# Cross-attention in a decoder layer: each projection in two halves, between the head pairs of twelve steps

## The reference

```python
q = einsum('oc,bct->bot', Wq, target) + bq      # target = layernorm(x), per batch 256 x 512
k = einsum('oc,bcs->bos', Wk, source) + bk      # source = ctx
v = einsum('oc,bcs->bos', Wv, source) + bv
dot = einsum('bhdt,bhds->bhts', q, k) / sqrt(16)
dot = mask * dot - (1 - mask) * 1e6
amap = softmax(dot, axis=-1) * mask
out = einsum('bhts,bhds->bhdt', amap, v)
x = x + out
```

## Time and profile before

| | us |
|---|---|
| median of 3 runs | 2342.87 (2342.37 to 2356.09) |
| profiled execution | 2321.17 |
| its span | 2319.4, mean granted clock 0.963 |
| PE busy | 2162.2 (93%) |
| DVE busy | 1597.9 (69%) |
| ACT busy | 797.5 (34%) |
| POOL busy | 759.0 (33%) |

### The profile page before, as it was taken

One profiled execution on the slowest core, in us unless ns is written; L12 is line 12 of the kernel. 1 busy time (PEld: TensorE's weight loads), 2 busy tenths in 40 slices (PEclk: granted clock), 3 DMA queues, 4 the chain that ended last, 5 costly groups with the idle time before them and its releaser, 6 DMA issues. The chain is left out here.

```text
span 2319.4 us, 35373 instructions
## 1 busy us (share of the span) xinstructions
PE 2162.2 (93%) x11638; PEld 1521.2 (66%) x11638; DVE 1597.9 (69%) x2873; ACT 797.5 (34%) x1843; POOL 759.0 (33%) x531
## 2 busy tenths in 40 slices
PE   6899999999999999999999998879899989789998
PEld 4677777777777777777777876423333333267776
DVE  7658878878876558878888875657867878542221
ACT  1223323323323333223323322235555556652221
POOL 3234335335345234334335333212122221122211
PEclk9899999999999999999999999888978998999999
DMA  5211011011012111011011004745565444311100
GB/s 205 80 48 52 15 51 51 16 49 51 16 49 100 56 47 53 7 58 51 9 56 51 26 10 72 121 79 98 103 104 97 68 91 80 101 59 55 55 36 19
DMA packets 58564, 141.87 MB, mean 61 GB/s; under 512 B 9022, under 2 KB 23558, under 8 KB 53478
## 3 DMA queue, kind: packets, MB, share of 16 engines
q1 hardware_dynamic: 56726, 138.42, 23.7%
q10 hardware_dynamic: 1744, 2.25, 0.3%
HBM read 89.53 MB, written 17.29 MB: 46 GB/s over the span
## 5 line engine op out<-in xcount | busy, mean ns | idle before, releaser
L1638 DVE TENSOR_REDUCE x_mx<-x_pm 128x1 f32<-128x512 f32 x512 | 317.6, 682 | 77.3 <-PE x_pm L1731 74.4
L1493 ACT ACTIVATE x_E<-x_pd 128x512 f32<-128x512 f32 x512 | 265.0, 603 | 178.4 <-PE x_pd L1745 177.3
L1091 PE MATMUL a_pj<-q_big,a_wqk_h 128*128 128x512 f32 x1024 | 290.0, 405 | 0.5 <-POOL a_wqk_l L631 0.5
L1107 PE MATMUL a_pj<-a_wvg_h,q_big 128*128 128x512 f32 x1024 | 285.6, 406 | 1.1 <-DVE a_rm L789 1.0
L1107 PEld LDWEIGHTS a_pj<-a_wvg_h,q_big 128*128 128x128 f32 x1024 | 185.2, 188 | 51.8 <-DVE a_rm L789 2.4
L789 DVE TENSOR_TENSOR a_rm<-a_pj,a_rope 128x1024 f32<-128x1024 f32 x128 | 155.7, 1218 | 78.8 <-PE a_pj L1091 77.5
L1091 PEld LDWEIGHTS a_pj<-q_big,a_wqk_h 128*128 128x128 f32 x1024 | 183.0, 188 | 40.3 <-POOL a_wqk_l L631 1.3
L520 ACT ACTIVATE a_v<-a_pj 128x256 f32<-128x256 f32 x128 | 49.2, 384 | 414.8 <-PE a_pj L1107 414.8
L663 POOL TENSOR_TENSOR a_ogl<-a_ogf,a_ogh 128x512 fp32r<-128x512 f32 x62 | 79.3, 1302 | 281.8 <-ACT a_ogf L557 281.8
L1759 PE MATMUL x_pa<-x_E,x_vx 128*32 128x512 f32 x1024 | 154.3, 678 | 0.0
L866 DVE TENSOR_TENSOR a_acc<-a_po,a_acc 128x512 f32<-128x512 f32 x128 | 86.0, 687 | 88.6 <-PE a_po L1220 88.6
(11 more groups left out here) (220 smaller groups left out, 4618.4 us busy)
## 6 DMA issues: line engine op xcount, KB each, us to landing
a_qk_raw<-in_wqk SPq DMA_DIRECT2D x16, 1024.0 KB, 5.3
a_vg_raw<-in_wvg SPq DMA_DIRECT2D x16, 1024.0 KB, 4.9
a_wo_raw<-in_wo SPq DMA_DIRECT2D x16, 512.0 KB, 3.6
x_Q<-x_hi SPq DMA_DIRECT2D x20, 256.0 KB
x_K<-x_hi SPq DMA_DIRECT2D x20, 256.0 KB
a_acc<-in_w SPq DMA_DIRECT2D x6, 704.0 KB, 4.3
a_wt<-in_w SPq DMA_DIRECT2D x24, 176.0 KB, 2.3
weights_scratch<-a_wt SPq DMA_DIRECT2D x24, 176.0 KB, 1.9
```

The lines of the kernel that those rows point to most:

```text
L1091: last = mm(pj[:, j % 2, :], wa[:, c, j * P:(j + 1) * P], xa[:, c, p * UT:(p + 1) * UT], start=k == 0, stop=k == 11)
L1107: last = mm(pj[:, tt % 2, :], xa[:, c, t0:t0 + P], wa[:, c, :], start=k == 0, stop=k == 11)
L1493: nc.scalar.activation(E[:, n % ESLOTS, :], pd[:, n % 3, :], ACT.Exp, scale=XD ** -0.5).then_inc(exp_done, 1)
L1638: nc.vector.reduce_max(mx[:, u % 2, at:at + 1], pm[:, k % 3, :], AX_X).then_inc(pm_done, 1)
```

## The change

- A projection is made in two parts (`project_part`, k = 0 and 1: for K and Q each is one of the two accumulated input tiles, for V one half of the columns). The twelve parts stand in steps 4 to 15, between the first two row scores and the second two dots.
- PE's `turn_max` goes behind the first two row scores of a quad instead of ahead of them, and the numbering of pm's banks follows. In DVE's step the maxima are taken two and two, with `max_rows` and `take_projection` between them. `take_projection` is in the odd steps 5 to 15.
- `norm_stats` goes to step 1, `norm` to step 6. `high` goes to steps 6, 8, 10 and 12, in the middle of the four exponentials.
- Inversions: one part a step, in steps 0, 2, 3, 4, 8, 10, 12 and 14 (n = 2b - 2 in steps 0 and 2, n = 2b - 1 in steps 3 to 10, n = 2b in steps 12 and 14).
- SP: x of the first three batches is loaded ahead of the loop and before the fills; x of batch b + 3 in step 15; the context of b + 2 in step 1; the fills run from step 9 to step 1 of the next batch (LATE has two); for batch 1 only the six fills of Q stand ahead of the loop, those of K in steps 1 to 3 of batch 0; stores in steps 5 and 13.
- POOL: `rsqrt` first, the order of the low parts and of `divide_and_add` changed.

```diff
--- before.py
+++ after.py
@@ -1357,11 +1357,14 @@
 
         def maxima_slot(u, q, i):
 
-            return 17 * u + 4 * q + i
+            k = 4 * q + i
+            return 17 * u + k - (u > 1 and k < 2)
 
         def turned_slot(u):
 
-            return 17 * u + 16
+            if u == 0:
+                return 16
+            return 17 * u + 18 - 2 * (u == QUADS - 1)
 
         def stacked(b):
 
@@ -1382,17 +1385,21 @@
         def inverses(b, G):
 
             if b + 2 < B:
-                due = {7: (-1, (0, 1)), 8: (-1, (2,)), 9: (-1, (3,)), 10: (0, (0,)), 11: (0, (1, 2)), 12: (0, (3,))}
+                due = {0: (-2, 2), 2: (-2, 3), 3: (-1, 0), 4: (-1, 1), 8: (-1, 2), 10: (-1, 3), 12: (0, 0), 14: (0, 1)}
+            elif b + 1 < B:
+                due = {0: (-2, 2), 2: (-2, 3), 3: (-1, 0), 4: (-1, 1), 8: (-1, 2), 10: (-1, 3), **{11 + i: (0, i) for i in range(4)}}
             else:
-                due = {**{2 + i: (-1, (i,)) for i in range(4)}, **{10 + i: (0, (i,)) for i in range(4)}}
-            n, parts = due.get(G, (0, ()))
-            return 2 * b + n, (parts if 2 * b + n >= 0 else ())
+                due = {**{3 + i: (-1, i) for i in range(4)}, **{10 + i: (0, i) for i in range(4)}}
+            n, part = due.get(G, (-2 * B, 0))
+            return 2 * b + n, ((part,) if 2 * b + n >= 0 else ())
 
         block = s.enter_context(nc.Block())
 
-        FILLS = {10: ((1, 0), (1, 1)), 11: ((1, 4), (1, 5)), 12: ((0, 0), (0, 1)), 13: ((0, 2),), 14: ((0, 3), (1, 2)), 15: ((1, 3), (0, 4))}
-        LATE = {0: ((0, 5),)}
-        WHOLE = tuple((w, k) for w in range(2) for k in range(6))
+        FILLS = {9: ((1, 0),), 10: ((1, 1), (1, 4)), 11: ((1, 5),), 12: ((1, 2), (1, 3)),
+                 13: ((0, 0),), 14: ((0, 1), (0, 2)), 15: ((0, 3),)}
+        LATE = {0: ((0, 4),), 1: ((0, 5),)}
+        FIRST = tuple((0, k) for k in range(6))
+        SECOND = {1: ((1, 0), (1, 1)), 2: ((1, 4), (1, 5)), 3: ((1, 2), (1, 3))}
 
         @block.sync
         def _(sp):
@@ -1408,7 +1415,8 @@
 
             sp.dma_start(mc[:], mask_cols).then_inc(const_in, 16)
             sp.dma_start(bv_t[:], bv.to_broadcast([P, 256])).then_inc(const_in, 16)
-            load_x(1)
+            for b in (1, 2, 0):
+                load_x(b)
 
             def mask_rows(b, e):
                 r = b % 3
@@ -1448,9 +1456,7 @@
             rows(0)
             mask_rows(1, 0)
             mask_rows(1, 1)
-            stack(1, WHOLE)
-            load_x(2)
-            load_x(0)
+            stack(1, FIRST)
             for t in range(QUADS):
                 b = t // 4
                 for q in range(4):
@@ -1460,18 +1466,18 @@
                         spread(t - 1)
                     if q == 1 and t + 1 < QUADS:
                         rows(t + 1)
-                    if b and G in (3, 15):
-                        store(2 * b - 2 + (G == 15))
-                    if b and b + 1 < B:
-                        stack(b + 1, LATE.get(G, ()))
+                    if b and G in (5, 13):
+                        store(2 * b - 2 + (G == 13))
+                    if b + 1 < B:
+                        stack(b + 1, (LATE if b else SECOND).get(G, ()))
                     if b + 2 < B:
-                        if G == 2 and b:
-                            load_x(b + 2)
-                        if G == 3:
+                        if G == 1:
                             load_c(b + 2)
                         if G in (6, 7):
                             mask_rows(b + 2, G - 6)
                         stack(b + 2, FILLS.get(G, ()))
+                    if G == 15 and b + 3 < B:
+                        load_x(b + 3)
                     if t >= QUADS - 6:
                         load_raw(4 * (t + 6 - QUADS) + q)
             spread(QUADS - 1)
@@ -1506,13 +1512,15 @@
                 high(1, j)
             for t in range(QUADS):
                 for q in range(4):
-                    for i in range(4):
-                        exponent(16 * t + 4 * q + i)
+                    G = 4 * (t % 4) + q
+                    exponent(16 * t + 4 * q)
+                    exponent(16 * t + 4 * q + 1)
+                    if G in (6, 8, 10, 12) and t // 4 + 2 < B:
+                        high(t // 4 + 2, order(2)[G // 2 - 3])
+                    exponent(16 * t + 4 * q + 2)
+                    exponent(16 * t + 4 * q + 3)
                     if q == 0 and t:
                         take_weighted(t - 1)
-                    G = 4 * (t % 4) + q
-                    if 8 <= G < 12 and t // 4 + 2 < B:
-                        high(t // 4 + 2, order(2)[G - 8])
             take_weighted(QUADS - 1)
 
         @block.gpsimd
@@ -1567,17 +1575,17 @@
             values(1, 1)
             clear(pool, spent)
             for b in range(B):
+                if b + 2 < B:
+                    rsqrt(b + 2)
                 if b:
                     divide_and_add(2 * b - 2)
                 if b + 2 < B:
-                    rsqrt(b + 2)
-                    low(b + 2, 2)
-                    low(b + 2, 3)
+                    for j in order(2)[0:3]:
+                        low(b + 2, j)
                 if b:
                     divide_and_add(2 * b - 1)
                 if b + 2 < B:
-                    low(b + 2, 0)
-                    low(b + 2, 1)
+                    low(b + 2, order(2)[3])
                     values(b + 2, 0)
                     values(b + 2, 1)
             divide_and_add(2 * B - 2)
@@ -1629,8 +1637,8 @@
                                             bv_t[:].rearrange("p (o n) -> p o n", o=1).to_broadcast([P, 2, 256]),
                                             ALU.add).then_inc(pp_done, 1)
 
-            def row_max(u, q):
-                for i in range(4):
+            def row_max(u, q, heads):
+                for i in heads:
                     k, at = maxima_slot(u, q, i), 8 * (i % 2) + 4 * (i // 2) + q
                     dve.wait_ge(pm_ready, k + 1)
                     if u >= 2 and q == 0 and i == 0:
@@ -1661,38 +1669,41 @@
                 nc.vector.tensor_tensor(xt[:, (B - 1) % 4, ct, :], att[:, ct], xt[:, (B - 1) % 4, ct, :], ALU.add).then_inc(x2_done, 1)
 
             dve.wait_ge(filled, 2)
-            row_max(0, 0)
-            row_max(0, 1)
+            row_max(0, 0, range(4))
+            row_max(0, 1, range(4))
             dve.wait_ge(const_in, N_CONST)
             take_projection(0, 4)
-            row_max(0, 2)
+            row_max(0, 2, range(4))
             take_projection(0, 5)
-            row_max(0, 3)
+            row_max(0, 3, range(4))
             take_projection(1, 0)
             max_rows(0)
             for q in range(4):
                 take_projection(1, q + 1)
-                row_max(1, q)
+                row_max(1, q, range(4))
             take_projection(1, 5)
             for t in range(QUADS):
                 b, u = t // 4, t + LEAD
                 for q in range(4):
+                    G = 4 * (t % 4) + q
+                    if u < QUADS:
+                        row_max(u, q, (0, 1))
                     if q == 0 and u <= QUADS:
                         max_rows(u - 1)
+                    if G in range(5, 16, 2) and b + 2 < B:
+                        take_projection(b + 2, order(2)[G // 2 - 2])
                     if u < QUADS:
-                        row_max(u, q)
-                    G = 4 * (t % 4) + q
+                        row_max(u, q, (2, 3))
                     n, parts = inverses(b, G)
                     for i in parts:
                         invert(n, i)
                     if b + 2 < B:
-                        if 5 <= G < 7:
-                            norm_stats(b + 2, G - 5)
-                        if G == 8:
+                        if G == 1:
+                            norm_stats(b + 2, 0)
+                            norm_stats(b + 2, 1)
+                        if G == 6:
                             norm(b + 2, 0)
                             norm(b + 2, 1)
-                        if 7 <= G < 13:
-                            take_projection(b + 2, order(2)[G - 7])
             invert_last()
 
         @block.tensor
@@ -1702,24 +1713,28 @@
             def bank(b, j):
                 return (pp, pa)[j % 2] if b < 2 else pp
 
-            def project(b, j):
-                if j == 0:
-                    after(pe, xn_done, 2 * b - 2)
-                if j == 2:
-                    pe.wait_ge(c_in, 16 * b)
-                after(pe, pp_done, projected(b, j) - (b < 2))
+            def project_part(b, j, k):
+                if k == 0:
+                    if j == 0:
+                        after(pe, xn_done, 2 * b - 2)
+                    if j == 2:
+                        pe.wait_ge(c_in, 16 * b)
+                    after(pe, pp_done, projected(b, j) - (b < 2))
                 dst = bank(b, j)
                 if j < 4:
                     w, src = ((wq_t, xn), (wk_t, cx))[j // 2]
```

(43 more changed lines are left out.)

## The result

| | before | after |
|---|---|---|
| median (us) | 2349.15 (2342.37 to 2356.09, 4 runs) | 2267.36 (2264.97 to 2268.49, 4 runs) |
| profiled execution, span | 2321.17, 2319.4 | 2267.18, 2265.4 |
| mean granted clock | 0.963 | 0.970 |

The ratio is 0.965, 95% interval 0.9611 to 0.9689: 3.5% faster.

The account below looks back on a forecast made before the run. Bound by a ring of waits between PE and DVE, with stalls and clock falls. Gains of 32 us (batches 1 to 5), 22 (batch 0) and 2 (batch 6) gave 2265 profiled, plus 21.7: 2287, range 2249 to 2322.

Parts of the forecast that it names:

- The ring: Cross-attention step: first score, maximum, fourth score, weighted sum and next dots wait on each other; 2.93 us a plain step.
- part 1: Cross-attention steps with a half projection take 3.25 us; a batch 54.1, bounds 53.7 (DVE's work) and 64.4.
- part 2: turn_max behind the first scores: worth a few tenths of a us, four times a batch, already in the 54.1.
- part 3: Row maxima at a batch's start: the stall shrinks from 1.3 to about 0.3 us.
- part 4: Transfer queue, batches 1 to 5: PE newly waits 2.3 us for the context in step 4, plus 0.9 refilling the ring.
- rival C: PE is the bound, each half costs its full 0.96 us: 64.8 a batch, 2299 us; chance 0.13.
- part 5: One clock fall a batch at the new stall, lasting 10 us and costing 5: a batch takes 62.6 us.
- part 6: Batch 0: row maxima no longer behind the moved loads; 57 us against 78.85, gain 22.
- part 7: Batch 6 gains 2 us (bounds 0 and 5); batch 7 and everything ahead of and behind the stage untouched.
- B: Batches 1 to 5: context in time, clock stays up; 54.9 us a batch, 2249 us; chance 0.21.
- D: Transfers come 5 us late, clock stays low as long as in batch 3; 2325 us, no change; chance 0.15.
- E: Context wait in step 4 drops the clock, low through the halves; slower, 2454 us with all twelve low; chance 0.09.

Follow-up runs that it names:

- e4: The changed kernel with each projection whole again, in odd steps 5 to 15 ahead of the weighted sum, DVE's take behind the four maxima; 2311.5 us, ratio 0.994.
- e6: e2 with the context in step 0, halves behind the fourth score ahead of the weighted sum, and DVE's take after the maxima; 2277.1 us, ratio 0.976.
- e12: e9 with each projection whole, in the odd steps, left between the two head pairs; 2249.1 us, ratio 0.966.
- e9: e2 with the context and then x issued in step 1, between the row maxima and the fills; 2235.2 us, ratio 0.956.
- e7: e2 with the context in step 0, turn_max ahead of a quad's first scores and banks numbered as in the kernel before; 2253.1 us, ratio 0.966.
- e1: The changed kernel with the statistics in step 3 instead of step 1, and POOL's first divide_and_add ahead of rsqrt; 2254.1 us, ratio 0.972.
- e3: The kernel before with only the changed start (x loaded first, only Q's six fills ahead of the loop); 2316.8 us, ratio 0.994.
- e2: The changed kernel with x of batch b + 2 loaded in step 2, statistics in step 4, divide_and_add ahead of rsqrt; 2243.0 us, ratio 0.967.
- e10: e2 with the row maxima and the context issued by ACT on its own queue; 2244.2 us, ratio 0.961.
- e11: The kernel before with e3's start and the row maxima issued by ACT; 2318.8 us, ratio 0.996.

## Why the prediction was right, point by point

- **The ring and the halves (part 1): right, the size a little off.** A half in the middle costs 0.52 of its 0.96 us (3.45 against 2.93), and e4, e6 and e12 show that it is the place first and the split second. I took 3.25 a step. The mis-sized terms are PE's: I let four pairs and the weighted sum be 2.0 to 2.3 and the half 0.96, and they came to 1.40 + 0.99 and 1.06, 3.45 in all. That is 2.4 us a batch, of which 0.9 came back, since the 0.3 that I added to each quad for the turned maxima cost nothing on top of 4 x 3.45. The bound of DVE's 53.7 held: e9's batches come to 55.7.
- **turn_max (part 2): right in its direction**, a few tenths forecast and 0.7 us a quad in the pace of e7, though not in its time.
- **Rows at the batch's start (part 3): right.** No such wait of over 0.2 us is left.
- **The queue (part 4): the backlog right, the waiter wrong.** I forecast PE waiting 2.3 us for the context in step 4. PE never waits for it, since DVE waits first, up to 5.5 us, for x in step 1. My own list of what stands ahead puts x and mask at about 1.4 + 1 + 14.7 - 2.1 + 1 + 3 + 1.7 = 20.7 after step 13 began; in batch 1 they landed 20.1 after it (1539.96 to 1560.07), and 3.0 after DVE asked for them. The list was right, and I had put the statistics into DVE's account of step 1 without asking for it. e1 takes that wait out, and there PE does wait 1.2 to 2.5 for the context and 1.5 to 2.9 for the rows. The recorded count has a slip that changes little: four steps without a half are put at 14.4 there and in rival C, where part 1's own figures give 14.2 with the turned maxima and 13.9 without.
- **The clock (part 5): right in size, 10 us of low level a batch forecast, and partly luck**, since I hung it on the wrong wait and it varies from trace to trace. Twice one minus the mean clock, times the length, gives 9.9, 7.4, 9.9, 7.3 and 14.2 in batches 1 to 5. A batch was forecast at 62.6 and the five take 62.3 in the mean: two errors that cancel, quads 1 to 3 longer by 1.5 together, quad 0 shorter by 1.8.
- **Batch 0 (part 6): right**, 58.2 against 57; e3 shows that the start alone gives 16.6 of the 20.6 us.
- **Batches 6 and 7 (part 7): right in batch 6**, 4.1 us won where I had 2 with bounds of 0 and 5. Behind it 7.4 were lost with a low clock in the last quads, where no row scores are left. I had called that stretch untouched; its code is, and since e1, e2 and e12 keep the clock there, the loss is not shown to come from the change. With the 3.0 ahead of the loop it is why 58 us won show as 54, near the 56 forecast.
- **From the profile to the median: wrong, and it is the 20 us between 2287 and 2267.** I carried the 21.7 us between the profiled execution and the median over as a constant. It isn't one: for the changed kernel it is 0.2. The kernel before scatters with its clock, in three runs of one job 2305.71 at 0.971, 2315.93 at 0.966 and 2333.09 at 0.956, while the changed kernel's four runs were at 0.970 to 0.972 and within 3.5 us. The profiled execution was one of the good ones of the kernel before and an ordinary one of the kernel after.
- **The rivals.** B (2249, nothing waits) is what e9 shows to be possible with another order of the queue: 55.7 a batch against 54.9 forecast for it. C is out by the 3.45 of the step and by e6 and e12. D and E did not occur: no low stretch lasted through the halves.

## What to carry to other kernels

When a step is moved ahead, walk through what it reads as well as what it delays: here the loads were costed for those behind them, and the one consumer that had itself been moved was the one to wait (DVE's statistics, 20.5 us). In a loop tied by waits in both directions, work put between two dependent pairs is cheaper than the same work where all engines have run dry (0.5 against 1.2 us a step here), so place first, then split; at the end the split brought nothing. Order a full queue by who is needed first, and take a move's effect on those it overtakes into the forecast. Here the kernel with fewer stalls also scattered less, and then the profile of one good run understates the gain. And compare traces stretch by stretch, to see whether a difference lies where the change is.

## What the runs showed of the hardware

- A step at the low clock takes 4.59 us instead of 2.93, so a kernel like this loses 0.36 us for each us at 1.2 GHz. In the changed kernel PE's waits of 4.0 to 6.6 us each came with 7 to 14 us of it; in the kernel before and e3 waits of 1.2 to 1.3 were followed by anything from none to 41 us. Waits of up to 0.98 us in batches 1 to 5 of e9 were followed by none. A long wait is not the only way into it: it came in e6 with none of over 0.4 us (above), and between 1930 and 1968 us of the changed kernel, and at the same place in e9, where PE has dots and weighted sums only and waits 0.2 to 0.55 us a step. In the kernel before and in e2 it did not come there. Why is open.
- Two matmuls of 54 rows on different row halves take 0.33 us together for 512 columns. Half a projection takes 1.06 us between two pairs, where half of a whole one's 1.91 would be 0.96.
- The context on ACT's queue landed no earlier than on SP's, though it was issued 2.5 us earlier (e10, batch 2), and rows of 4 KB alone on ACT's queue took 9 us (e11, batch 2).
